# Where the attention's stack loads are queued, how the last stage's loads are cut, and which engine writes constants

## The chip, the cores and the metric

The kernel runs on one core of a Trainium2 chip. The metric is the device time of one execution in microseconds; the median of the runs is compared. TensorE (PE) does matmuls, VectorE (DVE) and ScalarE (ACT) elementwise work, GpSimd (POOL) a part of it, and SyncE (SP) has no arithmetic and issues DMAs. ScalarE can issue DMAs as well, on a queue of its own. Each engine executes its own list in order and waits on semaphores.

## The reference, cut to what matters

Two residual layers on `x` (4 x 1024 x 512): a gated state-space layer (input projection, convolution over four taps, layer norm, a scan over 1024 positions, output projection) and then a modulated attention with 16 heads of 32 columns:

```python
x = x + _L0_cond_ref(x, cond_2048, ...)
# second layer, x (B, S, H) with styles s1, s2 of cond_2048
attn = jnp.einsum('bhqd,bhkd->bhqk', q, k) * scale
attn = jax.nn.softmax(attn, axis=-1)
out = jnp.einsum('bhqk,bhkd->bhqd', attn, v).transpose(0, 2, 1, 3).reshape(B, S, H)
out = jnp.einsum('bsh,oh->bso', out, w_weight) * w_dc[:, None, :]
x = x + out + skip
```

The change touches the attention and the last projection alone.

## The kernel before, in words

The program is a chain of stages with a barrier between them: `pre_phase`, `scan_phase`, `proj_phase` (until about 2297 us of the profile), `attention_phase` (until about 3287 us) and `out_phase` (to the end).

**The attention.** 16 groups `n` of four heads each (four groups a batch), each group two halves of 512 queries, each half eight steps of 128 keys: 256 steps `g`, 16 to a group. In step `g` TensorE computes the scores of heads 0 and 1 (L1182), the products with `v` of step `g-1` (L1192), the scores of heads 2 and 3, one of the row-maximum units `u` twelve steps ahead (`max_unit`, L1168), and a part of the sums over keys (`sum_keys`, L1207). ScalarE takes the exponential of each score tile (L1328); the score tiles have two banks, so the scores of head `h` wait for the exponential of head `h-2`. VectorE reduces each maximum unit (L1215). GpSimd adds the probabilities of two steps (L1354) and, from group 4 on, multiplies finished halves by the inverse sums of their batch (`scale_raw`, L1250), after its pair 5 and pair 7 of each group's eight.

The scores need the row maximum in one more row of `qs` (against a row of -1 in `ks`): after eight units VectorE turns the maxima of half `m` (L1224), and `send_max` (L1134) writes them with four small DMAs into row 96 of `qs`. `ks`, `qs` and `v` are rings of two: `load_stacks(n+1)` overwrites what group `n-1` used, in ten DMAs (three of 512 KB for `ks`, six of 256 KB for `qs`, one of 512 KB for `v`).

All DMAs of this stage are issued by SyncE, in the order of a list written by hand (L1264 to L1292). For group `n` it does: store the half that GpSimd scaled last (`store_o`), wait for `products` and issue `load_stacks(n+1)`, in each fourth group `store_rden` (waits for VectorE's last quarter of the inverse sums of the batch), `load_rd(m)` (inverse sums broadcast to 32 partitions; it waits for `rden_out` at a batch's first), `send_max(2n+1)`, `load_mats(n+2)` (inputs of the maximum units), `send_max(2n+2)`, `load_rd(m+1)`, `store_o(m)`, with `m = 2(n-4)` from group 4 on. A step that waits holds all behind it.

At the start VectorE clears `row_max` and writes -1 into row 96 of both `ks` buffers (L1336) before its first maximum; TensorE does twelve maximum units before the first scores and waits on `cleared` for those rows.

**The last stage.** 32 output tiles of 128 rows (L1422: four matmuls a tile, eight records each in the profile), 8 tiles a batch. Batch 0 of the attention's output is loaded at the attention's end; SyncE loads batch 1 (2 MB) with the first three `x2` tiles, sends the last batch's inverse sums, loads five `x2` tiles, waits for batch 1, and issues batches 2 and 3 (2 MB each) and `rd` (four of 512 KB). Only then comes the loop that stores tile `t` and loads `x2` tile `t+8`. VectorE scales a tile (L1437) into one of four buffers `o` and adds `x2` (L1429); the buffer of tile `t` must have been stored for tile `t-4`. Batch 3 is divided by its sums on VectorE (L1383) between the tiles of batch 2.

Of the kernel before, what the change touches and what calls it, by code (L numbers as in the profile page):

```python
# [1064 lines left out]
def attention_phase(nc, I, QK, V, OT, RD, WDC, w_out, w_row, mats, banks):  # L1065
# [17 lines left out]
    SCALE_AT = {5: 0, 7: 1}  # L1083
    LATER = 4
    QUARTERS = 4
    RING = 2
    LANES = NH * PER_BATCH
    with ExitStack() as ctx:
# [26 lines left out]
        def load_mats(sp, n):  # L1115
            for dst, part in ((qm[n % RING], 0), (km[n % RING], 2)):
                sp.dma_start(dst.bitcast(f32), QK[part].rearrange("b (g r) s -> (b g) r s", r=P)[n]).then_inc(mats_in[n % RING], 16)

        def load_stacks(sp, n):
            src = lambda part: QK[part].rearrange("b (g h p) s -> (b g) p h s", h=GROUP, p=HD)[n]  # L1120
            for row, part in enumerate((2, 3, 2)):
                sp.dma_start(ks[n % RING][row * HD:(row + 1) * HD].bitcast(f32), src(part)).then_inc(stacks_in[n % RING], 16)
            for half in range(NH):
                for row, part in enumerate((0, 0, 1)):
                    sp.dma_start(qs[n % RING][row * HD:(row + 1) * HD, half].bitcast(f32), src(part)[:, :, half * HALFQ:(half + 1) * HALFQ]).then_inc(stacks_in[n % RING], 16)
            sp.dma_start(v[n % RING][:], V[n].rearrange("(q p) c -> p q c", p=P)).then_inc(stacks_in[n % RING], 16)

        def send_max(sp, m):

# [123 lines left out]
        with nc.Block() as block:  # L1253
            @block.sync
            def _(sp):
                start_counts(sp, sems)
                load_stacks(sp, 0)
                sp.dma_start(lanes[:], I["lanes"]).then_inc(consts, 16)
                send_max(sp, 0)
                load_stacks(sp, 1)  # L1260
                sp.dma_start(w_out[:], I["w_t"].rearrange("(k p) n -> p k n", p=P)).then_inc(late_consts, 16)
                for b in range(BATCH):
                    sp.dma_start(w_row[:, b, :], WDC[1, b:b + 1, :].to_broadcast([P, MODEL])).then_inc(late_consts, 16)
                for n in range(NGROUPS):  # L1264
                    m = NH * (n - PER_BATCH)
                    if m >= 1:
                        store_o(sp, m - 1)
                    if NH * n > LAST:
                        store_o(sp, NH * n - 1)
                    if n and n + 1 < NGROUPS:  # L1270
                        sp.wait_ge(products, START + n * STEPS)
                        load_stacks(sp, n + 1)
                    if n and n % PER_BATCH == 0:
                        store_rden(sp, n // PER_BATCH - 1)
                    if m >= 0:
                        load_rd(sp, m)
                    send_max(sp, 2 * n + 1)
                    if n + 2 < NGROUPS:
                        sp.wait_ge(unit_max, START + (n + 1) * NH * UNITS)
                        load_mats(sp, n + 2)  # L1280
                    if n + 1 < NGROUPS:
                        send_max(sp, 2 * n + 2)
                    else:
                        sp.wait_ge(unit_scores, START + ALL_STEPS)
                        for i in range(LANES):
                            sp.wait_ge(raw_out[i], START + 16 * ((LANES - 1 - i) // SLOTS + 1))
                        sp.dma_start(mats[:].bitcast(f32), OT[0:PER_BATCH].rearrange("g p s -> p g s")).then_inc(first_in, 16)
                    if m >= 0:
                        load_rd(sp, m + 1)
                        store_o(sp, m)  # L1290
                    if NH * n >= LAST:
                        store_o(sp, NH * n)  # L1292
                store_o(sp, LAST - 1)
                store_o(sp, HALVES - 1)
                for i in range(SLOTS):
                    sp.wait_ge(raw_out[i], START + 16 * ((HALVES - 1 - i) // SLOTS + 1))
                sp.wait_ge(rden_out, START + (BATCH - 1) * RDENS)
                sp.wait_ge(late_consts, START + 16 * (1 + BATCH))
                sp.wait_ge(first_in, START + 16)
# [20 lines left out]
            @block.scalar  # L1320
            def _(act):
                for g in range(ALL_STEPS):
                    for h in range(GROUP):
                        if h == 0 and g >= 4:
                            act.wait_ge(products, START + g - 3)
                            act.wait_ge(paired, START + g // 2 - 1)
                        act.wait_ge(scores, START + g * GROUP + h + 1)
                        nc.scalar.activation(probs[:, g % 4, h, :], p_exp[h % 2], ACT.Exp).then_inc(exps, 1)  # L1328
                    if g and g % NQ == 0:
                        take_raw(act, g // NQ - 1)  # L1330
                take_raw(act, HALVES - 1)
            @block.vector
            def _(dve):
                for i in range(RING):
                    nc.vector.memset(row_max[i][:], 0.0)
                    nc.vector.memset(ks[i][KROWS:STACK].bitcast(f32), -1.0).then_inc(cleared, 1)  # L1336
                dve.wait_ge(cleared, START + RING)
                for u in range(ALL_STEPS):
                    dve_unit(dve, u)
                    if u % UNITS == UNITS - 1:  # L1340
                        dve_row(dve, u // UNITS)
                    batch, after = divmod(u + 1 - AHEAD - LATER, PER_BATCH * STEPS)
                    if batch > 0 and after == 0:
                        take_den(dve, batch - 1)
                    if batch > 0 and 1 <= after <= QUARTERS:
                        invert(dve, batch - 1, after - 1)
                dve.wait_ge(key_sums, START + BATCH * LANES * NQ)
            @block.gpsimd
            def _(pool):
                for t in range(ALL_STEPS // 2):  # L1350
                    pool.wait_ge(exps, START + 2 * (t + 1) * GROUP)
                    if t >= 2:
                        pool.wait_ge(key_sums, START + 2 * (t - 1))
                    nc.gpsimd.tensor_tensor(out=pair_sum[:, t % 2], in0=probs[:, (2 * t) % 4], in1=probs[:, (2 * t + 1) % 4], op=ALU.add).then_inc(paired, 1)  # L1354
                    batch, r = divmod(t, LANES * NQ // 2)
                    if batch and r % NQ in SCALE_AT:
                        scale_raw(pool, (batch - 1) * LANES + r // NQ * 2 + SCALE_AT[r % NQ])

def out_phase(nc, I, OT, RD, X2, w, w_row, first, banks, out):

    with ExitStack() as ctx:
# [9 lines left out]
        inverted = sem("inverted"); rden_out = sem("rden_out"); rd_in = sem("rd_in"); divided = sem("divided")  # L1371
        TILES = BATCH * NQ

        def load_batch(sp, b):
            sp.dma_start(ot[b][:], OT.rearrange("(b g) p s -> b p g s", b=BATCH)[b]).then_inc(b_in[b], 16)  # L1375
        def load_rd(sp, b):
            for h in range(P // HD):
                sp.dma_start(rd[h * HD:(h + 1) * HD].rearrange("p k s -> p (k s)"), RD[b, h:h + 1].rearrange("o l s -> o (l s)").to_broadcast([HD, NK * SEQ])).then_inc(rd_in, 16)  # L1378
        def divide(dve, b, k):
            if k == 0:  # L1380
                dve.wait_ge(b_in[b], START + 16)
                dve.wait_ge(rd_in, START + 64)
            nc.vector.tensor_tensor(out=ot[b][:, k, :], in0=ot[b][:, k, :], in1=rd[:, k, :], op=ALU.mult).then_inc(divided, 1)  # L1383
        def load_x2(sp, t):
# [2 lines left out]
        with nc.Block() as block:  # L1387
            @block.sync
            def _(sp):
                start_counts(sp, sems)  # L1390
                for t in range(3):
                    load_x2(sp, t)
                load_batch(sp, 1)
                sp.wait_ge(inverted, START + 1)
                for h in range(P // HD):
                    sp.dma_start(RD[BATCH - 1, h], rden[h * HD:h * HD + NH * NK, :]).then_inc(rden_out, 16)
                for t in range(3, NQ):
                    load_x2(sp, t)
                sp.wait_ge(b_in[1], START + 16)
                load_batch(sp, 2)  # L1400
                load_batch(sp, 3)
                sp.wait_ge(rden_out, START + P // HD * 16)
                load_rd(sp, BATCH - 1)
                for t in range(TILES):
                    sp.wait_ge(added, START + t + 1)
                    sp.dma_start(out[t // NQ, t % NQ * P:(t % NQ + 1) * P, :], o[:, t % 4, :]).then_inc(o_out[t % 4], 16)
                    if t + NQ < TILES:
                        load_x2(sp, t + NQ)
                for i in range(4):
                    sp.wait_ge(o_out[i], START + 16 * TILES // 4)  # L1410
            @block.tensor
            def _(pe):
                for t in range(TILES):
                    b, q = divmod(t, NQ)
                    if q == 0 and 0 < b < BATCH - 1:
                        pe.wait_ge(b_in[b], START + 16)
                    if t >= 4:
                        pe.wait_ge(scaled, START + t - 3)
                    for k in range(NK):
# [93 lines left out]
```

## Time and profile before

| | |
|---|---|
| median of 3 runs | 3407.75 us (3393.54 to 3408.2) |
| profiled execution | 3417.8 us |
| its span in the profile | 3416.0 us |
| mean granted clock of TensorE | 0.904 |
| busy: PE, DVE, ACT, POOL | 3042.5 us (89%), 2197.5 (64%), 1125.3 (33%), 1131.1 (33%) |
| SyncE's queue (q1), share of the 16 DMA engines | 39.1% |
| ScalarE's queue (q10) | 4.7% |

The profile is of one execution, slower than the median by 10 us. Its busy times say which engine is near its limit over the whole; a stretch of the timeline says where it stands still. "Granted clock" is the share of full speed (2.4 GHz) that TensorE was given: 0.50 is 1.2 GHz, and a value between is a mean over a stretch with both. The time to landing of a DMA counts from its issue. In the rows, `x4` after an operation means four of them in one entry, `<-` in brackets names what ended the idle time, and L with a number is a line of the kernel.

### The profile page before, as it was taken

Reading aid. Unit: us, or ns where it says so; the run is one execution under the profiler, and the core shown is the slowest. Engines: PE = TensorE matmul, PEld = TensorE weight load, DVE = VectorE, ACT = ScalarE, POOL = GpSimd, SP = SyncE. Lnnn points to the kernel's source line nnn. Section 1 sums busy time; section 2 is a strip of 40 time slices with the busy share of each in tenths; the row PEclk is TensorE's granted clock in tenths of the full one; section 3 lists DMA queues with packets and bytes.
Section 4 is the critical chain, followed back from the end, with each engine's and each line's share of the span. In section 5 each row is a group of like instructions: output and inputs, shape, how many; then the busy total and the mean of one; then the engine's idle time right before and its main releaser. Section 6 shows DMA issues by size and latency. Waiting matters only on the chain. (4 is left out here: it accounts for less than half of the span.)

```text
span 3416.0 us, 55584 instructions
## 1 busy us (share of the span) xinstructions
PE 3042.5 (89%) x20298; PEld 1427.7 (42%) x20298; DVE 2197.5 (64%) x3126; ACT 1125.3 (33%) x1944; POOL 1131.1 (33%) x462
## 2 busy tenths in 40 slices
PE   6888865599999999999984999987998998989989
PEld 3555544233444444444433666662332332323334
DVE  3766763488898988989844333437766665665614
ACT  3644542011111111111112112213665665655620
POOL 0111111112333343434302111003666665665630
PEclk9878865578999999999996999997999998988999
DMA  2233224435565555555543433344434343343354
GB/s 75 114 109 142 89 103 139 131 74 133 146 152 145 147 145 148 144 151 147 150 133 121 141 130 137 136 157 119 112 75 107 78 115 85 95 104 82 81 192 145
DMA packets 248554, 420.82 MB, mean 123 GB/s; under 512 B 51736, under 2 KB 117912, under 8 KB 242024
## 3 DMA queue, kind: packets, MB, share of 16 engines
q1 hardware_dynamic: 202344, 385.61, 39.1%
q10 hardware_dynamic: 46080, 33.57, 4.7%
q8 instruction: 70, 1.15, 0.1%
q14 instruction: 60, 0.49, 0.1%
HBM read 257.82 MB, written 160.98 MB: 123 GB/s over the span
## 5 line engine op out<-in xcount | busy, mean ns | idle before, releaser
L491 DVE CUSTOM_DVE_ANT_0 b_h<-b_h,b_bx,b_bounds_all 128x256 f32<-128x256 f32 x2048 | 966.7, 535 | 147.7 <-PE b_bx L604 147.7
L1215 DVE TENSOR_REDUCE e_half_max<-ef_banks 128x4 f32<-128x2048 f32 x256 | 586.1, 2293 | 320.5 <-PE ef_banks L1168 320.5
L1354 POOL TENSOR_TENSOR e_pair_sum<-e_probs 128x2048 f32<-128x2048 f32 x128 | 585.0, 4570 | 506.2 <-PE ef_banks L1207 302.0
L1328 ACT ACTIVATE e_probs<-ef_banks 128x512 f32<-128x512 f32 x1024 | 555.8, 595 | 405.8 <-PE ef_banks L1182 405.7
L1182 PE MATMUL ef_banks<-e_qs,e_ks 97*128 97x512 f32 x1024 | 397.7, 469 | 52.7 <-DMA e_qs<-e_max_t 48.8
L614 PE MATMUL b_y_psum<-b_h,b_c_weights 128*32 128x128 f32 x8224 | 344.9, 288 | 2.5 <-ACT b_y_stage L654 2.5
L1182 PEld LDWEIGHTS ef_banks<-e_qs,e_ks 97*128 97x128 f32 x1024 | 161.3, 197 | 399.0 <-ACT e_probs L1328 299.5
L604 PE MATMUL b_bx<-b_x_moving,b_b_weights 24*128 24x512 f32 x1024 | 265.7, 514 | 57.4 <-DMA b_x_moving<-xn_parts 45.2
L525 PE MATMUL b_gate<-b_w_gate,b_x_tile 128*128 128x512 f32 x512 | 309.0, 687 | 3.8 <-DMA b_w_gate<-in_w_in_t_dram 3.8
L654 ACT COPY b_y_stage<-b_y_psum 128x128 f32<-128x128 f32 x256 | 67.9, 265 | 734.9 <-PE b_y_psum L614 733.0
L1192 PE MATMUL ef_banks<-e_probs,e_v 128*32 128x512 f32 x2048 | 288.9, 638 | 0.4 <-ACT e_probs L1328 0.4
L534 PE MATMUL b_p_out<-b_w_out,b_yg_t 128*128 128x512 f32 x512 | 279.0, 637 | 10.3 <-ACT b_yg_t L547 10.3
L604 PEld LDWEIGHTS b_bx<-b_x_moving,b_b_weights 24*128 24x128 f32 x1024 | 97.9, 188 | 445.2 <-DVE b_h L491 397.9
L588 POOL TENSOR_TENSOR b_b_weights<-b_bd_all,b_mask_b 128x512 fp32r<-128x512 f32 x64 | 81.2, 1268 | 612.1 <-PE b_y_psum L614 531.9
L153 PE MATMUL a_p_rows<-a_x_t,a_w_in 128*128 128x512 f32 x512 | 247.8, 643 | 21.7 <-PEq L78 20.5
L614 PEld LDWEIGHTS b_y_psum<-b_h,b_c_weights 128*32 128x32 f32 x8224 | 200.1, 112 | 136.7 <-issue 83.0
L279 DVE SCALAR_TENSOR_TENSOR a_acc<-a_padded,a_w_conv,a_acc 128x1024 f32<-128x1024 f32 x96 | 165.7, 1726 | 110.3 <-ACT a_acc L226 108.0
L265 POOL TENSOR_TENSOR a_xn<-a_xn,a_ln_g 128x1024 f32<-128x1024 f32 x32 | 76.1, 2379 | 464.3 <-ACT a_xn L206 464.3
L1207 PE MATMUL ef_banks<-e_pair_sum,e_lanes 128*32 128x256 f32 (+1 forms) x2016 | 166.7, 404 | 3.3 <-POOL e_pair_sum L1354 2.7
L153 PEld LDWEIGHTS a_p_rows<-a_x_t,a_w_in 128*128 128x128 f32 x512 | 104.5, 209 | 146.4 <-issue 144.9
L1168 PE MATMUL ef_banks<-ef_mats 32*128 32x512 f32 x1024 | 137.0, 522 | 29.4 <-DVE e_half_max L1215 23.2
L784 POOL TENSOR_TENSOR d_xl<-d_x,d_s_row 128x512 f32<-128x512 f32 x32 | 47.9, 1504 | 336.5 <-DMA d_x<-x_tiles 336.5
(183 smaller groups left out, 3272.6 us busy)
## 6 DMA issues: line engine op xcount, KB each, us to landing
b_x_moving<-xn_parts SPq DMA_DIRECT2D x256, 128.0 KB
e_ks<-qk_parts SPq DMA_DIRECT2D x48, 512.0 KB, 7.6
e_qs<-qk_parts SPq DMA_DIRECT2D x96, 256.0 KB, 11.3
xn_full<-a_xn SPq DMA_DIRECT2D x32, 512.0 KB, 2.6
xn_parts<-a_hi SPq DMA_DIRECT2D x64, 256.0 KB, 2.4
xn_parts<-a_lo SPq DMA_DIRECT2D x64, 256.0 KB, 2.4
b_x_moving<-xn_parts SPq DMA_DIRECT2D x256, 64.0 KB
silu_gate<-b_sg ACTq DMA_DIRECT2D x64, 256.0 KB, 4.2
```

The costliest lines, as they stand in the source:

```text
L153: mm = nc.tensor.matmul(p_rows[m % 2][:, h * 512:h * 512 + 512], w_in[:, k, m * P:(m + 1) * P], x_t[:, k, h * 512:h * 512 + 512], start=(k ...
L491: return nc.vector._custom_dve(bass.dve_ops.TENSOR_ADD_SAT, **operands)
L525: mm = nc.tensor.matmul(gate[:], x_tile[:, k, :], w_gate[:, k, half * HALF:(half + 1) * HALF], start=(k == 0), stop=(k == NK - 1))
L534: mm = nc.tensor.matmul(p_out[:], yg_t[:, m, :], w_out[:, m, :], start=(m == 0), stop=(m == NM - 1))
L604: m = nc.tensor.matmul(bx[v % 2][:, r, :], b_weights[e * GROUP:e * GROUP + K, i, k, :], x_moving[e * GROUP:e * GROUP + K, i, k, :], start= ...
L614: m = nc.tensor.matmul(y_psum[32 * j:32 * j + 32, 0:128], c_weights[:, (u // T) % 2, u % T, :], h[:, u % RING, 128 * j:128 * j + 128], sta ...
L1182: nc.tensor.matmul(p_exp[h % 2], ks[i][:, h, kt * P:(kt + 1) * P], qs[i][:, half, h, :], start=True, stop=True).then_inc(scores, 1)
L1192: mm = nc.tensor.matmul(p_o[HD * h:HD * (h + 1), :], v[n % RING][:, kt, HD * h:HD * (h + 1)], probs[:, g % 4, h, :], start=(kt == 0), stop ...
L1207: mm = nc.tensor.matmul(p_d[HD * h:HD * (h + 1), cols], lanes[:, lane, :], pair_sum[:, t % 2, h, cols], start=(within == 0), stop=(within ...
L1215: nc.vector.tensor_reduce(out=half_max[:, u // UNITS % 2, :, r // NH, r % NH], in_=(banks[:, u % 2 * GROUP:(u % 2 + 1) * GROUP] if u < FIR ...
L1328: nc.scalar.activation(probs[:, g % 4, h, :], p_exp[h % 2], ACT.Exp).then_inc(exps, 1)
L1354: nc.gpsimd.tensor_tensor(out=pair_sum[:, t % 2], in0=probs[:, (2 * t) % 4], in1=probs[:, (2 * t + 1) % 4], op=ALU.add).then_inc(paired, 1)
```

## The change

In the attention, `load_stacks` is cut into `load_stack(e, n, piece)` with ten pieces, the same DMAs as before. For groups 0 and 1 SyncE issues them as before. For groups 2 to 15 ScalarE issues one piece in each of the steps 2 to 11 of the group before, behind the step's exponentials. SyncE's list is put in another order: `send_max(2n+1)` and `load_mats(n+2)` come first, then `store_rden`, then both `load_rd`. The memsets of row 96 of `ks` go from VectorE to GpSimd. In the last stage the loads of batches 1 to 3 and of `rd` are cut in four; those of batch 2, `rd` and batch 3 go one behind each of the tiles 0 to 11 of the store loop, and the wait for batch 1 on SyncE goes.

```diff
@@ -1083,6 +1083,8 @@
     SCALE_AT = {5: 0, 7: 1}
     LATER = 4
     QUARTERS = 4
+    PIECES = 10
+    ISSUE_FROM = 2
     RING = 2
     LANES = NH * PER_BATCH
     with ExitStack() as ctx:
@@ -1116,14 +1118,17 @@
             for dst, part in ((qm[n % RING], 0), (km[n % RING], 2)):
                 sp.dma_start(dst.bitcast(f32), QK[part].rearrange("b (g r) s -> (b g) r s", r=P)[n]).then_inc(mats_in[n % RING], 16)
 
-        def load_stacks(sp, n):
+        def load_stack(e, n, piece):
             src = lambda part: QK[part].rearrange("b (g h p) s -> (b g) p h s", h=GROUP, p=HD)[n]
-            for row, part in enumerate((2, 3, 2)):
-                sp.dma_start(ks[n % RING][row * HD:(row + 1) * HD].bitcast(f32), src(part)).then_inc(stacks_in[n % RING], 16)
-            for half in range(NH):
-                for row, part in enumerate((0, 0, 1)):
-                    sp.dma_start(qs[n % RING][row * HD:(row + 1) * HD, half].bitcast(f32), src(part)[:, :, half * HALFQ:(half + 1) * HALFQ]).then_inc(stacks_in[n % RING], 16)
-            sp.dma_start(v[n % RING][:], V[n].rearrange("(q p) c -> p q c", p=P)).then_inc(stacks_in[n % RING], 16)
+            if piece < 3:
+                dst, part = ks[n % RING][piece * HD:(piece + 1) * HD], src((2, 3, 2)[piece])
+                e.dma_start(dst.bitcast(f32), part).then_inc(stacks_in[n % RING], 16)
+            elif piece < 9:
+                half, row = divmod(piece - 3, 3)
+                dst, part = qs[n % RING][row * HD:(row + 1) * HD, half], src((0, 0, 1)[row])[:, :, half * HALFQ:(half + 1) * HALFQ]
+                e.dma_start(dst.bitcast(f32), part).then_inc(stacks_in[n % RING], 16)
+            else:
+                e.dma_start(v[n % RING][:], V[n].rearrange("(q p) c -> p q c", p=P)).then_inc(stacks_in[n % RING], 16)
 
         def send_max(sp, m):
 
@@ -1254,10 +1259,12 @@
             @block.sync
             def _(sp):
                 start_counts(sp, sems)
-                load_stacks(sp, 0)
+                for piece in range(PIECES):
+                    load_stack(sp, 0, piece)
                 sp.dma_start(lanes[:], I["lanes"]).then_inc(consts, 16)
                 send_max(sp, 0)
-                load_stacks(sp, 1)
+                for piece in range(PIECES):
+                    load_stack(sp, 1, piece)
                 sp.dma_start(w_out[:], I["w_t"].rearrange("(k p) n -> p k n", p=P)).then_inc(late_consts, 16)
                 for b in range(BATCH):
                     sp.dma_start(w_row[:, b, :], WDC[1, b:b + 1, :].to_broadcast([P, MODEL])).then_inc(late_consts, 16)
@@ -1267,17 +1274,15 @@
                         store_o(sp, m - 1)
                     if NH * n > LAST:
                         store_o(sp, NH * n - 1)
-                    if n and n + 1 < NGROUPS:
-                        sp.wait_ge(products, START + n * STEPS)
-                        load_stacks(sp, n + 1)
+                    send_max(sp, 2 * n + 1)
+                    if n + 2 < NGROUPS:
+                        sp.wait_ge(unit_max, START + (n + 1) * NH * UNITS)
+                        load_mats(sp, n + 2)
                     if n and n % PER_BATCH == 0:
                         store_rden(sp, n // PER_BATCH - 1)
                     if m >= 0:
                         load_rd(sp, m)
-                    send_max(sp, 2 * n + 1)
-                    if n + 2 < NGROUPS:
-                        sp.wait_ge(unit_max, START + (n + 1) * NH * UNITS)
-                        load_mats(sp, n + 2)
+                        load_rd(sp, m + 1)
                     if n + 1 < NGROUPS:
                         send_max(sp, 2 * n + 2)
                     else:
@@ -1286,7 +1291,6 @@
                             sp.wait_ge(raw_out[i], START + 16 * ((LANES - 1 - i) // SLOTS + 1))
                         sp.dma_start(mats[:].bitcast(f32), OT[0:PER_BATCH].rearrange("g p s -> p g s")).then_inc(first_in, 16)
                     if m >= 0:
-                        load_rd(sp, m + 1)
                         store_o(sp, m)
                     if NH * n >= LAST:
                         store_o(sp, NH * n)
@@ -1328,13 +1332,16 @@
                         nc.scalar.activation(probs[:, g % 4, h, :], p_exp[h % 2], ACT.Exp).then_inc(exps, 1)
                     if g and g % NQ == 0:
                         take_raw(act, g // NQ - 1)
+                    n, s = divmod(g, STEPS)
+                    if 0 < n < NGROUPS - 1 and ISSUE_FROM <= s < ISSUE_FROM + PIECES:
+                        if s == ISSUE_FROM:
+                            act.wait_ge(products, START + n * STEPS)
+                        load_stack(act, n + 1, s - ISSUE_FROM)
                 take_raw(act, HALVES - 1)
             @block.vector
             def _(dve):
                 for i in range(RING):
                     nc.vector.memset(row_max[i][:], 0.0)
-                    nc.vector.memset(ks[i][KROWS:STACK].bitcast(f32), -1.0).then_inc(cleared, 1)
-                dve.wait_ge(cleared, START + RING)
                 for u in range(ALL_STEPS):
                     dve_unit(dve, u)
                     if u % UNITS == UNITS - 1:
@@ -1347,6 +1354,8 @@
                 dve.wait_ge(key_sums, START + BATCH * LANES * NQ)
             @block.gpsimd
             def _(pool):
+                for i in range(RING):
+                    nc.gpsimd.memset(ks[i][KROWS:STACK].bitcast(f32), -1.0).then_inc(cleared, 1)
                 for t in range(ALL_STEPS // 2):
                     pool.wait_ge(exps, START + 2 * (t + 1) * GROUP)
                     if t >= 2:
@@ -1371,14 +1380,13 @@
         inverted = sem("inverted"); rden_out = sem("rden_out"); rd_in = sem("rd_in"); divided = sem("divided")
         TILES = BATCH * NQ
 
-        def load_batch(sp, b):
-            sp.dma_start(ot[b][:], OT.rearrange("(b g) p s -> b p g s", b=BATCH)[b]).then_inc(b_in[b], 16)
-        def load_rd(sp, b):
-            for h in range(P // HD):
-                sp.dma_start(rd[h * HD:(h + 1) * HD].rearrange("p k s -> p (k s)"), RD[b, h:h + 1].rearrange("o l s -> o (l s)").to_broadcast([HD, NK * SEQ])).then_inc(rd_in, 16)
+        def load_rows(sp, b, k):
+            sp.dma_start(ot[b][:, k, :], OT[b * NK + k]).then_inc(b_in[b], 16)
+        def load_rd(sp, b, h):
+            sp.dma_start(rd[h * HD:(h + 1) * HD].rearrange("p k s -> p (k s)"), RD[b, h:h + 1].rearrange("o l s -> o (l s)").to_broadcast([HD, NK * SEQ])).then_inc(rd_in, 16)
         def divide(dve, b, k):
             if k == 0:
-                dve.wait_ge(b_in[b], START + 16)
+                dve.wait_ge(b_in[b], START + 64)
                 dve.wait_ge(rd_in, START + 64)
             nc.vector.tensor_tensor(out=ot[b][:, k, :], in0=ot[b][:, k, :], in1=rd[:, k, :], op=ALU.mult).then_inc(divided, 1)
         def load_x2(sp, t):
@@ -1390,22 +1398,25 @@
                 start_counts(sp, sems)
                 for t in range(3):
                     load_x2(sp, t)
-                load_batch(sp, 1)
+                for k in range(NK):
+                    load_rows(sp, 1, k)
                 sp.wait_ge(inverted, START + 1)
                 for h in range(P // HD):
                     sp.dma_start(RD[BATCH - 1, h], rden[h * HD:h * HD + NH * NK, :]).then_inc(rden_out, 16)
                 for t in range(3, NQ):
                     load_x2(sp, t)
-                sp.wait_ge(b_in[1], START + 16)
-                load_batch(sp, 2)
-                load_batch(sp, 3)
                 sp.wait_ge(rden_out, START + P // HD * 16)
-                load_rd(sp, BATCH - 1)
                 for t in range(TILES):
                     sp.wait_ge(added, START + t + 1)
                     sp.dma_start(out[t // NQ, t % NQ * P:(t % NQ + 1) * P, :], o[:, t % 4, :]).then_inc(o_out[t % 4], 16)
                     if t + NQ < TILES:
                         load_x2(sp, t + NQ)
+                    if t < NK:
+                        load_rows(sp, 2, t)
+                    elif t < 2 * NK:
+                        load_rd(sp, BATCH - 1, t - NK)
+                    elif t < 3 * NK:
+                        load_rows(sp, 3, t - 2 * NK)
                 for i in range(4):
                     sp.wait_ge(o_out[i], START + 16 * TILES // 4)
             @block.tensor
@@ -1413,7 +1424,7 @@
                 for t in range(TILES):
                     b, q = divmod(t, NQ)
                     if q == 0 and 0 < b < BATCH - 1:
-                        pe.wait_ge(b_in[b], START + 16)
+                        pe.wait_ge(b_in[b], START + 64)
                     if t >= 4:
                         pe.wait_ge(scaled, START + t - 3)
                     for k in range(NK):
```

## Rows read from the trace of the kernel before

**Rows 1.** Waits from 2180 us on: who, for whom: total us, times, longest.

```profile
PE ef_banks L1182 <- DMA e_qs<-e_max_t: 48.8, 11, 10.5
PE ef_banks L1422 <- DVE f_o L1437: 10.2, 1, 10.2
```

**Rows 2.** Stretches: ends, length, busy by engine, PEclk, DMA share, GB/s.

```profile
2320.00:2325.00 5.00, 1.96 (x12) 0.88 (x12) 5.00 (x4) 0.00 (x0) 0.00 (x0) 0.50 0.13 35
2355.00:2541.40 186.40, 186.39 (x1336) 61.35 (x1332) 131.17 (x70) 124.46 (x232) 127.73 (x29) 1.00 0.35 83
2541.40:2607.50 66.10, 55.43 (x381) 18.06 (x380) 41.44 (x26) 35.76 (x67) 36.60 (x9) 0.92 0.33 77
2629.00:2641.00 12.00, 12.00 (x87) 3.95 (x86) 8.57 (x6) 7.94 (x15) 7.82 (x3) 1.00 1.04 222
2778.00:2846.50 68.50, 57.84 (x380) 18.56 (x380) 41.42 (x25) 35.63 (x67) 38.94 (x11) 0.88 0.35 86
3024.10:3095.50 71.40, 60.72 (x381) 19.29 (x380) 41.45 (x25) 35.74 (x67) 39.02 (x11) 0.83 0.34 83
```

**Rows 3.** Timeline of TensorE: start us, us, engine, line, operation, [idle before <-releaser].

```profile
2590.09 1.22 PE L1182 MATMUL ef_banks<-e_qs,e_ks 97*128 97x512 f32 x2 [10.46 <-DMA e_qs<-e_max_t]
2648.26 1.01 PE L1182 MATMUL ef_banks<-e_qs,e_ks 97*128 97x512 f32 x2 [3.07 <-DMA e_qs<-e_max_t]
```

**Rows 4.** Timeline of SyncE's queue in the attention, columns as before.

```profile
2381.43 2.41 SPq L1134 DMA_DIRECT2D e_qs<-e_max_t  x4
2541.43 2.41 SPq L1134 DMA_DIRECT2D e_qs<-e_max_t  x4
...
2582.28 1.30 SPq L1156 DMA_DIRECT2D inverse_sums<-e_rden  x4
2586.49 2.40 SPq L1134 DMA_DIRECT2D e_qs<-e_max_t  x4
...
2624.93 1.39 SPq L1122 DMA_DIRECT2D e_ks<-qk_parts  x3
2630.77 8.88 SPq L1151 DMA_DIRECT2D e_rd<-inverse_sums  x4
2639.69 2.40 SPq L1134 DMA_DIRECT2D e_qs<-e_max_t  x4
...
3242.38 2.41 SPq L1134 DMA_DIRECT2D e_qs<-e_max_t  x4
```

**Rows 5.** DMA issues, 2624 to 2650 us: count, KB each, us to landing.

```profile
e_qs<-e_max_t SPq DMA_DIRECT2D x4, 2.0 KB, 6.2
```

**Rows 6.** Timeline of one undisturbed attention step, ScalarE.

```profile
2469.72 1.08 ACT L1328 ACTIVATE e_probs<-ef_banks 128x512 f32<-128x512 f32 x2 [0.67 <-PE ef_banks L1182]
```

**Rows 7.** Timelines: ScalarE and its queue in the scan; SyncE's queue.

```profile
725.87 0.36 ACTq L543 DMA_DIRECT2D silu_gate<-b_sg  x1
726.33 0.27 ACT L654 COPY b_y_stage<-b_y_psum 128x128 f32<-128x128 f32 x1 [0.62 <-ACT b_sg L541]
...
2395.55 3.18 SPq L1125 DMA_DIRECT2D e_qs<-qk_parts  x6
```

**Rows 8.** Timeline of the attention's start, VectorE and TensorE.

```profile
2301.09 3.47 DVE L1336 MEMSET e_ks<- 1x4096 f32 x1 [0.89 <-PE ef_banks L1168]
2309.11 17.67 DVE L1215 TENSOR_REDUCE e_half_max<-ef_banks 128x4 f32<-128x2048 f32 x8
...
2336.07 1.22 PE L1182 MATMUL ef_banks<-e_qs,e_ks 97*128 97x512 f32 x2 [3.59 <-DVE e_half_max L1215]
```

**Rows 9.** Groups by line, GpSimd: busy us, mean ns, idle before.

```profile
L1354 POOL TENSOR_TENSOR e_pair_sum<-e_probs 128x2048 f32<-128x2048 f32 x128 | 585.0, 4570 | 506.2 <-PE ef_banks L1207 302.0 <-ACT e_probs L1328 204.2
```

**Rows 10.** The chain that ended last, in order of time: start us, us, what.

```profile
3302.95 22.66 DMA out_dram<-f_o
```

**Rows 11.** Busy time in stretches of the last stage, columns as in Rows 2.

```profile
3287.00:3316.30 29.30, 29.30 (x64) 12.67 (x64) 7.89 (x8) 0.00 (x0) 0.00 (x0) 0.94 0.94 318
3326.50:3411.50 85.00, 84.95 (x192) 37.32 (x192) 38.45 (x57) 0.00 (x0) 0.00 (x0) 0.97 0.45 151
```

## The prediction, made before the result was known

> **What bounds the kernel now.** I read the page first: TensorE (PE) is busy 89% of the span, and no other engine is near it, so only time in which PE stands still or runs at the low clock can be won. The table of waits for the part from the attention on says where PE stands still [rows 1]: 48.8 us, in 11 waits of up to 10.5 us, for the DMA that writes the row maxima into `qs`, and 10.2 us in one wait, in the last stage, for VectorE's scaled tile. Next the stretches of the attention [rows 2]: while nothing stalls, the granted clock is 1.00; a stretch that should be two halves long (53.3 us) takes 66.1, 68.5 and 71.4 us at the three batch ends, with the clock at 0.92, 0.88 and 0.83. So a stall is paid twice, as idle time and as matmuls at 1.2 instead of 2.4 GHz after it: the first stretch is 12.8 us too long and holds a 10.46 us wait [rows 2, 3].
>
> Why the maxima are late is in SyncE's queue [rows 4]. Until 2541 us a send follows every 26.67 us (160.00 us from 2381.43 to 2541.43, six halves). Two things break this. At a batch end SyncE waits for the inverted sums (issued 2582.28) and their landing before it sends at 2586.49 maxima that the grid had ready at 2568.1; PE resumes at 2590.09 [rows 3, 4]. In other groups the ten stack loads go out at 2624.93 to 2630.7, the four `rd` loads behind them take 8.88 us to issue because the queue is full, the maxima go at 2639.69, and even then land 6.2 us after issue [rows 4, 5], so PE stands 3.07 us [rows 3]. Between sends 2541.43 and 3242.38 lie 23 halves: 613.3 us by the grid, 700.95 in fact, 87.6 us lost.
>
> **The attention's queues.** The change takes the ten loads off SyncE and sends `2n+1` before the waits for sums and `rd`. Followed on the grid of group 4 (step 3.33 us, group from about 2553): the odd maxima are ready at 2568.1 and now nothing is ahead of them, since `store_o(m-1)` needs a product that GpSimd finishes about step 2. PE wants them at step 8, 2580, a lead of 10 us. Then `load_mats` (two issues), the sums at 2582.28 as before (1.30 us), their landing and the first four `rd` issues until 2586.5 as before, four more by 2588.9 (at the 0.60 us that a send takes), and the even maxima come at 2594.8: SyncE is there 6 us early [rows 4]. `store_o(m)` still blocks SyncE until GpSimd is through, but what stands behind it (the odd maxima of the next group) is ready only at step 4. Both `rd` loads land before step 12, where GpSimd first wants one. So all 11 stalls go, and with them the low clock behind each; every dip of the clock here follows such a stall. I take the whole 87.6 us. What is late next is nothing of SyncE's: PE's own work of 53.3 us a group (busy share 100% in the undisturbed stretch [rows 2]).
>
> **The stacks on ScalarE.** 14 groups x 10 = 140 DMA issues, in steps 2 to 11, behind the four exponentials of the step. Behind a waiting or slow issue stand the next step's exponentials, and PE waits for those. The wait on `products` at step 2 is for a step that ended two steps before and costs nothing. ScalarE is idle 0.67 us between the fourth exponential of a step and the first of the next [rows 6]. An issue costs 0.36 us on ScalarE's queue, with the next instruction 0.10 us behind its end [rows 7], and 0.53 us each for the `qs` pieces on SyncE's (3.18 us for 6) [rows 7]. 0.36+0.10 fits the 0.67 us; 0.53+0.10+0.05 before it fills it just. Room on PE's side is small: the fourth head's weights load about when the second exponential ends, so what sticks out of the gap is paid nearly in full. At step 8 (piece 6) the copy of 0.59 us stands in the same gap, so up to 0.5 us sticks out in 14 steps, 7 us. Lower bound: 0, if the sequencer issues while the exponential still runs; below 0 is excluded, since nothing of ScalarE's becomes shorter. Upper bound: the whole issue, 140 x 0.53 = 74 us. I take 3 us, near the lower end, by the 0.36 us row, which is ScalarE's own. Transfer: the stacks moved at 222 GB/s at a full DMA share [rows 2]; a 256 KB piece is then 1.2 us and a 512 KB piece 2.4 us in a step of 3.33, so pieces don't pile up, and the last lands before step 13 against a need at 16.
>
> Beside this stands a rule that speaks against the change: the Trainium skill, DMA: Bandwidth & Descriptors, section "Issuing engines are not separate DMA queues", says that transfers started by several engines run on the same 16 DMA engines and interleave, so that another issuer saves issue time alone. By that rule the queue gains only the issue order, and with the burst unchanged the maxima could still land late; since the pieces here are also spread over ten steps, it does not change the sum.
>
> **The start of the attention.** VectorE's two one-partition memsets (3.47 us each, with 0.89 us before each) hold its first maximum until 2309.11 [rows 8]. Without them it starts when PE's first unit is done, about 2301.1 by what the first memset's row names: 8.0 us earlier. The 12 maxima behind run back to back (17.67 us for 8) and gate PE's first score at 2336.07, which moves to 2328.0. What else gates it: the first stacks (the DMA share falls to 0.13 after 2320 [rows 2]), the first maxima sent about 2319 and landed by 2323, and GpSimd's memsets. The trace has none of that size on GpSimd: at the 2.23 ns per column of its additions (4570 ns for 2048 [rows 9]) two of 4096 take 18.3 us and end about 2318.4; at VectorE's price, 7 us. Only above 13.9 us each do they gate PE, which I exclude. Gain 8.0 us (bounds 0 and 8.7).
>
> **The last stage.** SyncE issues 4 MB of `ot` and 2 MB of `rd` ahead of the first output tile; that tile's DMA takes 22.66 us from 3302.95 [rows 10], VectorE waits for its buffer, PE stands 10.2 us [rows 1], and the 85.0 us that follow run at 0.97 [rows 11], 2.6 us of them lost to the clock. Now 512 KB go behind each of twelve tiles. The first store then has only the five `x2` tiles before it (1.25 MB at 318 GB/s [rows 11], 4 us), lands by about 3307, and is wanted by PE's ninth tile at 3316. Per tile some 1 MB (store, `x2`, piece) is 3.2 us at that rate, against 3.5 us of PE; batch 2 is in by tile 5 and wanted at 16, batch 3 by tile 13 and wanted at 17. The first batch's load costs three more issues, 1.3 us on SyncE, in front of nothing that PE waits for. Gain 10.2+2.6 = 12.8 us (bounds 0 and 13.5).
>
> **Sum.** 87.6+8.0+12.8 = 108.4 less 3 is 105.4 us. The profiled execution took 3417.8 us (span 3416.0): it becomes 3312.4, span 3310.6. It was 10 us above the median of 3407.75, and the runs spread over 15 us; taken off the median, 3302.
>
> **Rivals.**
> 1. ScalarE's issues lie on the path, with 0.53 us each: 74 us back instead of 3, 3373. For: ScalarE is in order and its exponentials gate PE. Against: the gap of 0.67 us.
> 2. The batch ends keep their stalls, because the even maxima stay behind sums and `rd`: 12.8+15.2+18.1 = 46 us less gain, 3348. Against: the 6 us of lead above.
> 3. The last stage keeps its stall, the pieces standing before the stores instead of the whole: 3315.
> 4. Slower: an issue on ScalarE blocks as SyncE's did when its queue was full, 8.88/4 = 2.2 us each [rows 4]. 140 x (2.22-0.67) = 217 us of exponentials late, less 108.4: 3516. It decides from 0.67+108.4/140 = 1.44 us an issue on. Against: SyncE put ten such pieces out in 5.8 us before anything blocked, and here one or two are in flight.
> 5. The change doesn't do what it says: the maxima still land late, because pieces and `mats` fill the engines in front of them. One piece is 2.4 us against 10 us of lead; with half the stalls kept, 3346.
>
> **Chances.** Forecast (3290 to 3312) 0.66; rival 1 in full or part 0.12; 2 with 5, 0.09; 3 0.07; 4 0.03; nothing gained within 0.5% (17 us, about what a measurement can tell) 0.03. The range reaches over rivals 3, 2 and 5, 3286 to 3348, and leaves out rival 1 in full and rival 4. Faster 0.94, same 0.03, slower 0.03.
>
> **What would show it.** Right: no PE wait on the maxima's DMA; sends every 26.67 us to the end; clock 1.00 through the attention; ScalarE's issues of 0.36 to 0.53 us with the step still 3.33 us in steps 2 to 11; VectorE's first maximum 1 us behind PE's first unit, not 9, and PE's first score 27 us behind it; no PE wait in the last stage, which is 111 to 112 us of PE. Wrong: steps 2 to 11 longer than the others (rival 1), a wait of about 10 us at steps 64, 128, 192 (rival 2), issues over 1.4 us (rival 4).

## The result

The changed kernel takes 3297.82 us (median of 4, 3292.41 to 3310.05) against 3406.03 us; the ratio is 0.9695, 95% interval 0.9658 to 0.9731. Forecast was 3302, from 105.4 us less; the medians are 108.2 us apart. The profiled execution (3292.41 us, span 3290.4) is 125.6 us shorter than the one before, but 20.6 us of that lie ahead of the attention, in stages whose code is the same: their first maximum unit starts at 2279.49 instead of 2300.07 us. What the change touches is compared by stage, from the first maximum unit to the first matmul of the last stage, and from there to the end:

| | before | after | difference |
|---|---|---|---|
| first unit to first score | 36.0 | 27.8 | -8.2 |
| first score to second send of maxima | 18.8 | 20.5 | +1.8 |
| second send to last send (30 halves) | 887.6 | 801.6 | -86.0 |
| last send to last stage | 44.6 | 44.6 | 0 |
| last stage | 129.0 | 116.4 | -12.6 |

The sum is 105.0 us. The row of 86.0 us can be split. Before, the stretch between the second and the last send reads

```profile
2354.82:3242.38 887.56, 838.10 (x5731) 272.44 (x5728) 574.18 (x315) 535.12 (x991) 575.62 (x143) 0.94 0.38 91
```

and the stretches after are these, with the columns of [rows 2]; the second is the attention between those sends:

```profile
2307.30:2327.80 20.50, 20.22 (x72) 6.78 (x72) 9.56 (x6) 10.10 (x19) 6.80 (x2) 0.59 0.86 225
2327.80:3129.40 801.60, 800.96 (x5730) 264.30 (x5726) 574.27 (x316) 535.13 (x991) 576.41 (x143) 1.00 0.38 100
3129.40:3174.00 44.60, 37.80 (x269) 12.13 (x269) 0.00 (x0) 25.81 (x48) 32.32 (x9) 0.96 0.25 83
3174.00:3290.40 116.40, 111.85 (x256) 49.23 (x256) 49.15 (x69) 0.00 (x0) 0.00 (x0) 0.98 0.64 217
```

TensorE's busy time for the same matmuls falls from 838.1 to 801.0 us, 37 us at the low clock that are gone, and with them go the 48.8 us of waits. The granted clock, 0.92, 0.88 and 0.83 at the batch ends before [rows 2], is 1.00 between these sends. The waits of TensorE from the first score on (two of 0.4 and 0.3 us, there before too, are left out): the two of [rows 1] are gone, nothing has come in their place.

```profile
PE ef_banks L1433 <- PEq L1258: 3.7, 1, 3.7
PE ef_banks L1187 <- DVE e_half_max L1220: 3.6, 1, 3.6
PE ef_banks L1212 <- POOL e_pair_sum L1363: 2.7, 1, 2.7
PE ef_banks L1212 <- DVE e_den L1235: 0.6, 3, 0.2
```

SyncE's queue around the first batch end, which answers to [rows 4]: sends follow at 26.67 us (27.12 over the batch end), the sums are no longer ahead of the odd maxima, and SyncE is done with the eight `rd` issues at 2562.5, 5.7 us before the even maxima (6 were forecast).

```profile
2541.13 2.40 SPq L1139 DMA_DIRECT2D e_qs<-e_max_t  x4
2543.58 1.45 SPq L1119 DMA_DIRECT2D ef_mats<-qk_parts  x2
2555.30 1.31 SPq L1161 DMA_DIRECT2D inverse_sums<-e_rden  x4
2558.80 3.71 SPq L1156 DMA_DIRECT2D e_rd<-inverse_sums  x8
2568.25 2.42 SPq L1139 DMA_DIRECT2D e_qs<-e_max_t  x4
2572.00 13.67 SPq L1147 DMA_DIRECT2D attended<-e_raw  x2
2594.92 2.40 SPq L1139 DMA_DIRECT2D e_qs<-e_max_t  x4
```

One step of ScalarE with a piece in it, against [rows 6, 7]: the issue begins at 2374.57, between the third and the fourth exponential's start, and is over before the fourth ends; the gap behind the fourth stays 0.67 us.

```profile
2374.32 0.60 ACT L1332 ACTIVATE e_probs<-ef_banks 128x512 f32<-128x512 f32 x1 [0.49 <-PE ef_banks L1187]
2374.57 0.34 ACTq L1125 DMA_DIRECT2D e_ks<-qk_parts  x1
2374.82 0.59 ACT L1332 ACTIVATE e_probs<-ef_banks 128x512 f32<-128x512 f32 x1
2376.08 1.09 ACT L1332 ACTIVATE e_probs<-ef_banks 128x512 f32<-128x512 f32 x2 [0.67 <-PE ef_banks L1187]
```

The start, against [rows 8]: GpSimd's two memsets take 3.5 us each (3.47 on VectorE) beside VectorE's maxima.

```profile
2279.45 6.95 POOL L1358 MEMSET e_ks<- 1x4096 f32 x2 [137.64 <-POOLq L904]
2280.33 17.68 DVE L1220 TENSOR_REDUCE e_half_max<-ef_banks 128x4 f32<-128x2048 f32 x8 [0.68 <-PE ef_banks L1173]
2307.30 1.22 PE L1187 MATMUL ef_banks<-e_qs,e_ks 97*128 97x512 f32 x2 [3.60 <-DVE e_half_max L1220]
```

The last stage, TensorE before and after, and the landing of the first output tile, which took 22.66 us before [rows 10]: the wait is gone, and the last 24 tiles take 82.6 us instead of 85.0.

```profile
3326.54 84.95 PE L1422 MATMUL ef_banks<-ef_w_out,f_ot 128*128 128x512 f32 x192 [10.24 <-DVE f_o L1437]
3203.30 82.56 PE L1433 MATMUL ef_banks<-ef_w_out,f_ot 128*128 128x512 f32 x192
out_dram<-f_o SPq DMA_DIRECT2D x1, 256.0 KB, 3.4
```

### The profile page after: what moved, and what is told of

It reads as the page before. It is cut to its first block and busy times, and to the rows that moved or that the text cites. A ratio compares the mean times of both kernels' runs of the same rounds, so it can differ in the third digit from the quotient of the medians.

```text
span 3290.4 us, 55593 instructions
## 1 busy us (share of the span) xinstructions
PE 2982.5 (91%) x20298; PEld 1411.0 (43%) x20298; DVE 2189.8 (67%) x3124; ACT 1125.0 (34%) x1944; POOL 1138.7 (35%) x464
## 5 line engine op out<-in xcount | busy, mean ns | idle before, releaser
L1187 PE MATMUL ef_banks<-e_qs,e_ks 97*128 97x512 f32 x1024 | 383.7, 454 | 3.9 <-DVE e_half_max L1220 3.6
L604 PE MATMUL b_bx<-b_x_moving,b_b_weights 24*128 24x512 f32 x1024 | 263.7, 510 | 54.8 <-DMA b_x_moving<-xn_parts 43.7
L525 PE MATMUL b_gate<-b_w_gate,b_x_tile 128*128 128x512 f32 x512 | 300.6, 670 | 3.8 <-DMA b_w_gate<-in_w_in_t_dram 3.8
L1197 PE MATMUL ef_banks<-e_probs,e_v 128*32 128x512 f32 x2048 | 275.4, 610 | 0.4 <-ACT e_probs L1332 0.4
```

The costliest lines, as they stand in the source:

```text
L525: mm = nc.tensor.matmul(gate[:], x_tile[:, k, :], w_gate[:, k, half * HALF:(half + 1) * HALF], start=(k == 0), stop=(k == NK - 1))
L604: m = nc.tensor.matmul(bx[v % 2][:, r, :], b_weights[e * GROUP:e * GROUP + K, i, k, :], x_moving[e * GROUP:e * GROUP + K, i, k, :], start= ...
L1187: nc.tensor.matmul(p_exp[h % 2], ks[i][:, h, kt * P:(kt + 1) * P], qs[i][:, half, h, :], start=True, stop=True).then_inc(scores, 1)
L1197: mm = nc.tensor.matmul(p_o[HD * h:HD * (h + 1), :], v[n % RING][:, kt, HD * h:HD * (h + 1)], probs[:, g % 4, h, :], start=(kt == 0), stop ...
```

## The experiments

Lengths of stages are taken from each kernel's own trace as above; "attention" is from the first maximum unit to the last stage: 986.9 us before, 894.5 after. "Between the sends" is from the second send of maxima to the last: 887.6 us before, 801.6 after. The kernels that keep stalls vary there from trace to trace: `out_only` and `memset_only`, whose code in that stretch is that of the kernel before, took 893.7 and 879.5 us, so a difference against the one trace before is good to some 8 us. The code cuts are shortened; `...` and words stand for what is left out.

**1. One part alone, on the kernel before.** `order_only` (SyncE's list for a group, shortened; the first line is as before):

```diff
  if n and n + 1 < NGROUPS: sp.wait_ge(products, ...); load_stacks(sp, n + 1)
+ send_max(sp, 2 * n + 1); load_mats(n + 2); store_rden; load_rd(m); load_rd(m + 1); send_max(2 * n + 2)
```

> The kernel before with SyncE's list alone in the new order; the ten stack loads stay on SyncE, ahead of send_max(2n+1). Theory A (the order is the cause: the sums and rd stood before the maxima): the burst is issued about 6 us into the group, drains in 16 us, so the maxima queued behind it land about 23 us into the group and PE wants them at 26.7; no stall at all is left, the attention loses all 86 us, sends every 26.67 us, 3320. Theory B (the burst on SyncE's queue is the cause in the inner groups): the three batch ends go (46 us), the eight waits of 1 to 3 us and their low clock stay (41 us), 3360.

Measured: 3325.3 us, ratio 0.977 (0.9731 to 0.9809), attention 911.1, 75.8 less. Theory A, nearly: all waits at batch ends are gone, but not all waits. Seven small ones remain, 5.2 us together. Between the sends it takes 811.7 us, 10.2 more than the changed kernel: those waits, and 4.8 us of longer busy time. SyncE's queue and TensorE show where a wait comes from: behind the burst the four small sends take 5.29 us to issue instead of 2.41 and land a median 7.1 us after issue.

```profile
2663.48 5.29 SPq L1134 DMA_DIRECT2D e_qs<-e_max_t  x4
```

```profile
2675.05 0.73 PE L1182 MATMUL ef_banks<-e_qs,e_ks 97*128 97x512 f32 x2 [0.51 <-DMA e_qs<-e_max_t]
```

Six of the seven waits are of 0.35 to 0.82 us, and the granted clock behind them stays 1.00. The seventh, of 1.78 us, ends at 3107.68, and this is the stretch with it:

```profile
3107.00:3113.00 6.00, 5.32 (x20) 1.70 (x24) 0.97 (x2) 2.56 (x5) 3.60 (x1) 0.53 0.02 6
```

`act_only` (the ScalarE part of the diff, `load_stacks` struck from SyncE's list, which otherwise keeps its old order):

> The kernel before with the stack loads on ScalarE, a piece a step, and SyncE's order as it was otherwise (sums, rd, then send_max(2n+1)). Both theories: the three batch ends keep their waits of 10.5 us and the low clock behind them, 46 us. Inner groups: rd is issued at once and the odd maxima in time, so the eight small waits go, 41 us, 3365. If the issues on ScalarE cost what the prediction's rival has (0.53 us each), the group gets 5.3 us longer and the time is 3440.

Measured: 3362.81 us, ratio 0.9876 (0.9847 to 0.9905), attention 942.9, 44.0 less. TensorE's waits on the maxima are the three at the batch ends alone:

```profile
PE ef_banks L1196 <- DMA e_qs<-e_max_t: 31.4, 3, 10.5
```

That is what both theories expected (3365). Order and ScalarE overlap: 75.8 and 44.0 alone, 86.0 together, all between the sends. Moving the loads to ScalarE takes all waits out of the inner groups, the order all but 5.2 us of them, and only the order takes out those of the batch ends. `act_only` moves the loads to another queue and spreads them as well; no run tells these two apart in the old order.

`out_only` (`out_phase` of the changed kernel) and `memset_only` (the memsets on GpSimd):

> The kernel before with the last stage of the changed one. By the sum 12.8 us less (10.2 wait and 2.6 low clock), 3394; by the rival that the pieces stand before the stores, nothing, 3407.

> The kernel before with the memsets of ks on GpSimd. PE's first score comes 8 us earlier after the stage's first maximum unit (27.9 us instead of 36.0), 3399 to 3400. If the first stacks or the first maxima's landing gate instead, less than 8 us, with PE's wait on a DMA there.

Measured: 3391.71 us, ratio 0.9956 (0.9926 to 0.9987), last stage 116.5 instead of 129.0; and 3403.87 us, ratio 1.000 (0.997 to 1.003), first score after 27.8 us instead of 36.0. The second can't be told in the total, and is plain in the stage.

**2. What an issue on ScalarE costs.** The changed kernel with 2, 5 and 10 pieces a step, as here with 5:

```diff
- if 0 < n < NGROUPS - 1 and ISSUE_FROM <= s < ISSUE_FROM + PIECES:
+ if 0 < n < NGROUPS - 1 and ISSUE_FROM <= s < ISSUE_FROM + PIECES // 5:
-     load_stack(act, n + 1, s - ISSUE_FROM)
+     for piece in range((s - ISSUE_FROM) * 5, (s - ISSUE_FROM + 1) * 5): load_stack(act, n + 1, piece)
```

> The changed kernel with two pieces of the stacks a step on ScalarE, in steps 2 to 6. In the changed kernel's trace an issue takes 0.32 us and starts while the last exponentials run, and the queue is idle for 1.1 us more before the next exponential starts. Theory A (issues overlap the exponentials; what is free is 1.45 us a step): two take 0.75 us, no cost, attention 894.5 us. Theory B (they must fit the 0.67 us gap behind the fourth exponential): 0.17 us too long in 5 steps of 14 groups, 12 us more, 906.

> As before with five pieces a step, in steps 2 and 3. Theory A: 5 x 0.37 = 1.85 us against 1.45, 0.4 us late in 28 steps, 11 us, attention 906. Theory B: 1.3 us late in 28 steps, 37 us, attention 931. If the engines' backlog of 1.3 MB a step delays the maxima as SyncE's burst did, PE has small waits on the maxima's DMA too.

> As before with all ten pieces at step 2. Theory A: 3.7 us against 1.45, 2.2 us late in 14 steps, 31 us, attention 926. Theory B: 3.2 us late, 45 us, attention 940. If ScalarE's queue blocks when full as SyncE's did (2.2 us an issue), up to 22 us in 14 steps, over 300 us more. The maxima of the second half leave at step 4.5, 8 us behind the burst, on another queue: if a queue of one's own keeps them out of the backlog, they land in 2 us; if the 16 engines work in order of issue, they land about 8 us later, still before step 8.

Measured: two, 3299.11 us (ratio 0.9691, 0.9643 to 0.9740), attention 895.0; five, 3320.12 us (0.9755, 0.9717 to 0.9793), 913.2; ten, 3376.2 us (0.9924, 0.9898 to 0.9949), 980.1. Two cost nothing (0.5 us): theory A. Five cost 18.7 us, between A's 11 and B's 37; ten cost 85.6, more than either. Both had the price of one issue too low (one alone 0.34 us, in a row near 0.5).

With five, TensorE's waits on ScalarE and the stretch between the sends are

```profile
PE ef_banks L1187 <- ACT e_probs L1332: 14.8, 28, 0.7
2323.86:3147.99 824.13, 809.23 (x5730) 265.67 (x5726) 574.17 (x315) 535.43 (x991) 576.89 (x143) 1.00 0.40 98
```

so the cost there is 22.6 us: the waits of 0.40 to 0.74 us, and some 8 us of matmuls that take longer although the granted clock stays 1.00 (two score matmuls behind a wait take 0.98 us instead of 0.73). Before the first piece is issued, from the first score to the second send, this trace is 3.9 us shorter than the changed kernel's, 16.7 instead of 20.5 us at a granted clock of 0.80 instead of 0.59; that is why the attention is only 18.7 us longer.

With ten, ScalarE, TensorE and a stretch of one burst, then the waits and the stretch between the sends:

```profile
2378.98 0.34 ACTq L1125 DMA_DIRECT2D e_ks<-qk_parts  x1
2379.24 0.59 ACT L1332 ACTIVATE e_probs<-ef_banks 128x512 f32<-128x512 f32 x1
2379.36 0.93 ACTq L1125 DMA_DIRECT2D e_ks<-qk_parts  x2
2380.32 3.25 ACTq L1129 DMA_DIRECT2D e_qs<-qk_parts  x6
2383.60 0.46 ACTq L1131 DMA_DIRECT2D e_v<-v_groups  x1
2384.18 1.09 ACT L1332 ACTIVATE e_probs<-ef_banks 128x512 f32<-128x512 f32 x2 [4.35 <-issue]
```

```profile
2384.83 1.28 PE L1187 MATMUL ef_banks<-e_qs,e_ks 97*128 97x512 f32 x2 [3.22 <-ACT e_probs L1332]
```

```profile
2384.00:2390.00 6.00, 5.17 (x24) 1.77 (x24) 2.69 (x3) 3.26 (x6) 1.98 (x1) 0.50 1.03 216
```

```profile
PE ef_banks L1187 <- ACT e_probs L1332: 43.7, 14, 3.2
2332.26:3219.43 887.17, 843.40 (x5732) 273.29 (x5728) 574.25 (x315) 535.57 (x991) 576.78 (x143) 0.95 0.38 91
```

The ten issues end 5.08 us after they began, TensorE stands 3.22 us, and then works at 1.2 GHz for the next 6 us. The 14 waits are 43.7 us; TensorE's busy time between the sends is 42.4 us longer than in the changed kernel, at a mean granted clock of 0.95. This half of the cost stood in neither theory. The waits alone come out at B's 45, but two and five pieces speak against B, and A with 5.1 us for ten instead of 3.7 comes near them too. The ten issues took 5.1 us, as SyncE's ten took 5.8 [rows 4]; on SyncE only the issues behind the ten were slow, and on ScalarE none follows, so whether its queue would slow an eleventh was not put to the test. The maxima in the same burst, on the other queue (DMA view, 2375 to 2400 us, last column us to landing):

```profile
e_qs<-e_max_t SPq DMA_DIRECT2D x4, 2.0 KB, 6.8
```

They were issued 5.6 us behind the burst. That is as late as the 6.2 us of [rows 5], where the burst was on the same queue and had ended 9 us before. TensorE did not wait for them, since they left early enough. So a queue of their own does not take the maxima out of the engines' backlog; this agrees with the Trainium skill, DMA: Bandwidth & Descriptors, "Issuing engines are not separate DMA queues".

**3. Is ScalarE needed?** `sp_later`: no issue on ScalarE, and in SyncE's list (shortened)

```diff
  send_max(sp, 2 * n + 1)
  load_mats(sp, n + 2)
+ if n and n + 1 < NGROUPS: wait products; all ten load_stack(sp, n + 1, piece)
```

> The changed kernel with the ten stack loads back on SyncE, in one burst, but behind send_max(2n+1) and load_mats instead of ahead of them. Theory A (what counts is what stands ahead of a send, in SyncE's list and in the engines' backlog, not whose queue it is): the burst is issued from step 4.5 on, drains until about step 11, the rd loads behind it are issued slowly but before step 11, and the even maxima at step 12.5 find the queue free; no wait on the maxima, attention 894.5 us, as with ScalarE. Theory B (a burst on SyncE's queue always costs, since rd behind it blocks SyncE at some 2 us an issue): the even maxima or rd come late in some groups, waits of PE on the maxima's DMA or on GpSimd's sums, attention 900 to 940.

Measured: 3312.79 us, ratio 0.9714 (0.9663 to 0.9765), attention 894.4, the changed kernel's to 0.1 us; no wait on the maxima, which landed after 2.4 us at most (5.3 in the changed kernel). The total is some 15 us above the changed kernel's because the stages ahead of the attention end later (2299.6 us instead of 2279.5 in the profiled executions). Theory A. The block is there (`rd`, 10.96 us), but ends 6.7 us before the next send:

```profile
2615.00 2.41 SPq L1139 DMA_DIRECT2D e_qs<-e_max_t  x4
2617.45 1.05 SPq L1119 DMA_DIRECT2D ef_mats<-qk_parts  x2
2618.56 1.43 SPq L1125 DMA_DIRECT2D e_ks<-qk_parts  x3
2620.03 3.47 SPq L1129 DMA_DIRECT2D e_qs<-qk_parts  x6
2623.54 0.43 SPq L1131 DMA_DIRECT2D e_v<-v_groups  x1
2624.02 10.96 SPq L1156 DMA_DIRECT2D e_rd<-inverse_sums  x8
2641.67 2.40 SPq L1139 DMA_DIRECT2D e_qs<-e_max_t  x4
```

**4. A shorter start.** `first10`, on the changed kernel, then the same with `sp_later`, beside the changed kernel again:

```diff
- FIRST = AHEAD
+ FIRST = AHEAD - 2
  scores_of(pe, g, (0, 1))
+ if g < AHEAD - FIRST: one more max_unit
```

> The changed kernel with 10 instead of 12 maximum units ahead of the first score; the two others follow in steps 0 and 1. By the start's arithmetic the first score moves from 27.8 to about 23.2 us behind the first unit, gated by the landing of the first maxima (issued at 19.0, 2.5 us of issue, 1.7 to land) and no longer by VectorE; attention 890. If the two late units hold PE in the slow first steps instead, the gain is given back there and the attention stays at 894.5.

> The changed kernel once more, beside the next one on the same chip. The stages ahead of the attention are those of the kernel before and have started the attention anywhere from 2279 to 2308 us so far, so the total may move by 15 us; the attention stays 894.5 us and the last stage 116.4.

> Stack loads on SyncE behind send_max(2n+1) and load_mats, and 10 instead of 12 maximum units ahead of the first score. If both hold together, the attention takes 890.1 us, 4.3 less than in the changed kernel, and in the total 4 us less, which may be too little to tell. If the stacks of group 2 and the two late units get in each other's way, there is a wait on the maxima in group 1.

Measured: `first10` 3305.7 us, ratio 0.9703 (0.9668 to 0.9739), first score after 23.4 us, attention 890.2; `after_again` 3305.0 us, 0.9698 (0.9674 to 0.9723), attention 894.5, last stage 116.4; `sp_first10` 3296.33 us, 0.9663 (0.9637 to 0.9689), attention 890.1, last stage 116.9. The late units hold TensorE 1.25 us twice, inside the gain. By the stages `sp_first10` is 4 us better than the changed kernel; the intervals of the totals overlap, so they don't show it.

## Why the prediction was right

- **Attention's queues**, 87.6 forecast, 86.0 measured between the same sends. The mechanism held: the order for the batch ends, and the burst for the inner groups (`act_only` left only the batch ends' 31.4 us of waits). The 1.6 us not gained are a term that the grid of 26.67 us left out: three sends across a batch end follow after 27.1 us, where TensorE waits 0.2 us for `e_den`. With the new order neither spreading nor a second queue is needed: the bursts of `sp_later` and `act_burst` make no wait on the maxima. That SyncE's queue was full stays a reading: the rows show 2.2 us for a `rd` issue behind the burst and 0.46 without one ahead (3.71 us for 8).
- **ScalarE**, 3 forecast, 0 measured: `sp_later` without any issue there has the same attention to 0.1 us. This step of the prediction failed, at a size that hardly counts. Its reasoning had the issue fit the gap behind the fourth exponential, while it runs beside the exponentials. Even at step 8, with the copy in the gap, nothing sticks out. The 0.53 us an issue of rival 1 is right for issues in a row, and was charged in a place where it is hidden.
- **Start**, 8.0 forecast, 8.2 measured (8.2 in `memset_only` too). In the steps after it 1.8 us come back, a term that was missing. It is not shown to come from the memsets: from the first score to the second send it is 18.7 us before at a granted clock of 0.68, 20.5 after at 0.59, and 16.7 in `memset_only` at 0.81, with the same work. Why the clock rises earlier or later there stays open. GpSimd's memset was bounded by 9.1 us and took 3.5.
- **Last stage**, 12.8 forecast, 12.6 measured, 12.5 alone. The first output tile landed 3.4 us after issue, where 4 were forecast.
- **The sum** was right to 0.4 us in the stages, and 3 us from the medians' difference. That closeness is partly luck: 1.6 us too much for the queues and 1.8 missing at the start stand against the 3 charged to ScalarE. Against the 879.5 and 893.7 us of `memset_only` and `out_only`, the queues would have gained 78 or 92 us instead of 86.
- **Untouched stages.** The stages ahead of the attention ended anywhere from 2279.4 to 2307.6 us over the profiles of all these kernels, with one code. This makes most of the spread of the totals; where stalls are left, the attention adds to it.

## What to carry to other kernels

In a hand-written DMA list, ask of each small transfer that gates the bound engine what stands ahead of it: waits in the list, issues that are slow behind a burst (2.2 us each here instead of 0.46), and bytes on the way. Moving the big loads behind it was worth as much as moving them to another engine. Price a stall with what the granted clock shows behind it: 48.8 us of waits cost 86 in all here, while 28 waits of 0.40 to 0.74 us left the clock at 1.00. And read a gain of a few us from the stage's length, not from the total.

## What the hardware showed that was not expected

- A DMA issue on ScalarE runs while its own exponentials do: two a step cost 0.5 us in all of the attention, five cost 22.6 between the sends.
- Without stalls the attention is reproducible: 894.5, 894.5 and 894.4 us in three traces (the changed kernel twice, `sp_later`). With them the stretch between the sends took 887.6, 893.7 and 879.5 us with the same code, though the waits sum to 48.8, 51.5 and 51.3 us. The clock behind a wait of 1 to 3 us differs: before, the wait of 1.12 us that ends at 2704.31 is followed by 6 us at 1.00, that of 1.62 us at 2759.33 by 6 us at 0.66.
- A one-partition memset of 4096 elements takes GpSimd 3.51 us; VectorE's rows show 3.47, each with 0.89 us of idle time before it [rows 8].
